# Adding x on GpSimd image by image, three images later, with each image stored alone

## What is computed

```python
g  = (x - mean) / sqrt(var + 1e-5)         # per image and channel (group norm with 32 groups of 1 channel)
xd = concat(g[..., 0::2, 0::2], g[..., 0::2, 1::2], g[..., 1::2, 0::2], g[..., 1::2, 1::2])  # 128 x 32 x 32
feats = concat(dwconv1x1(xd), dwconv3x3(xd), dwconv5x5(xd))   # depthwise, 3 x 128 channels
y   = einsum('bchw,oc->bohw', feats, w_proj)                  # 384 -> 128 channels
out = x + interleave(y)                                        # the inverse of the step to xd
```

## Time and profile before

| | us |
|---|---|
| median of 3 runs (lowest to highest) | 147.44 (147.08 to 148.12) |
| the profiled execution | 148.02 |
| its span, first to last instruction | 146.2 |
| busy: PE / DVE / POOL / ACT | 129.3 / 125.1 / 111.5 / 109.1 |
| granted TensorE clock, mean of the span | 0.955 of full |

### The profile page before, as it was taken

The page is one execution under the profiler, slowest core; times in us unless marked ns, Lnnn a source line. Parts: engine busy times, 40 slices in busy tenths (PEclk is TensorE's granted clock), DMA queues, the critical chain, the costliest instruction groups (busy, mean ns, idle before and its releaser), DMA issues.

```text
span 146.2 us, 1541 instructions
## 1 busy us (share of the span) xinstructions
PE 129.3 (88%) x507; PEld 97.5 (67%) x507; DVE 125.1 (86%) x153; ACT 109.1 (75%) x113; POOL 111.5 (76%) x81
## 2 busy tenths in 40 slices
PE   5963999999999999999999999999999996996500
PEld 5941878887877677767776777677766773783200
DVE  7467838989999999999999999999999999997700
ACT  1377973999999999999999999899989970500000
POOL 6110686979999999997989998999999999992000
PEclk9998579999999999999999999999999999999965
DMA  3999999707034034025019995700399920094997
GB/s 72 255 241 197 198 206 209 118 15 141 2 76 78 0 74 83 0 57 95 0 31 184 205 194 116 152 0 0 72 215 173 209 57 0 4 215 97 200 192 157
DMA packets 35799, 16.78 MB, mean 115 GB/s; under 512 B 34000, under 2 KB 34128, under 8 KB 35408
## 3 DMA queue, kind: packets, MB, share of 16 engines
q1 hardware_dynamic: 30928, 8.67, 31.0%
q0 software_dynamic: 1440, 7.04, 24.8%
q10 hardware_dynamic: 3424, 0.98, 3.3%
HBM read 5.46 MB, written 4.19 MB: 66 GB/s over the span
## 4 chain that ended last, share of the span: by engine, by line
PE 55%; DVE 17%; POOL 8%; DMA 7%; ACT 3%; issue 3%; ACTq 1%; DVEq 0%; POOLq 0%
PE YP L665 49%; DVE ACC L592 11%; POOL RING_SUM L316 7%; DMA X<-in_x_dram 7%; PE YP L716 6%; DVE F L602 3%; DVE ACC L584 2%; DVE ACC L596 2%; ACT HI L382 2%; ACT Y L413 1%; ACT PROD L430 1%; POOL LO L303 1%; DVEq L95 0%; DVE X L626 0%; ACTq L217 0%
## 5 line engine op out<-in xcount | busy, mean ns | idle before, releaser
L316 POOL TENSOR_TENSOR RING_SUM<-RING_SUM,PROD 128x900 f32<-128x900 f32 (+1 forms) x44 | 89.1, 2037 | 5.1 <-ACT PROD L430 0.8
L592 DVE SCALAR_TENSOR_TENSOR ACC<-G,coef,ACC 128x930 f32<-128x930 f32 (+1 forms) x60 | 71.6, 1194 | 1.9
L430 ACT ACTIVATE PROD<-G,coef 128x900 f32<-128x900 f32 (+1 forms) x44 | 43.7, 1057 | 0.0
L665 PE MATMUL YP<-HI,whi 128*128 128x512 f32 (+1 forms) x144 | 38.8, 425 | 3.1 <-ACT HI L382 3.1
L665 PE MATMUL YP<-HI,wlo 128*128 128x512 f32 (+1 forms) x144 | 38.3, 419 | 0.0
L665 PE MATMUL YP<-LO,whi 128*128 128x512 f32 (+1 forms) x144 | 36.9, 407 | 0.0
L665 PEld LDWEIGHTS YP<-HI,whi 128*128 128x128 f32 x144 | 29.1, 204 | 11.5 <-ACT HI L382 3.0
L665 PEld LDWEIGHTS YP<-HI,wlo 128*128 128x128 f32 x144 | 27.3, 190 | 9.2 <-issue 2.9
L665 PEld LDWEIGHTS YP<-LO,whi 128*128 128x128 f32 x144 | 27.2, 190 | 7.7 <-issue 1.0
L392 ACT ACTIVATE G<-X,nbias,rstd 64x1024 f32<-64x1024 f32 x16 | 21.1, 1318 | 3.8 <-DVE nbias L503 3.2
L413 ACT ACTIVATE Y<-YP 64x1024 f32<-64x1024 f32 x14 | 15.3, 1091 | 7.0 <-PE YP L716 6.7
(11 more groups left out here) (61 smaller groups left out, 64.3 us busy)
## 6 DMA issues: line engine op xcount, KB each, us to landing
LO<-G POOLq DMA_DIRECT2D x7, 543.0 KB, 4.9
X<-in_x_dram SPq DMA_DIRECT2D x14, 256.0 KB, 5.4
X<-Y POOLq DMA_DIRECT2D x3, 1024.0 KB, 7.0
out_dram<-X SPq DMA_DIRECT2D x12, 256.0 KB, 4.7
out_dram<-X SPq DMA_DIRECT2D x6, 128.0 KB, 3.1
XS<-in_x_dram SPq DMA_DIRECT2D x2, 256.0 KB, 4.3
X<-in_x_dram ACTq DMA_DIRECT2D x2, 256.0 KB, 8.2
XS<-in_x_dram SPq DMA_DIRECT2D x1, 512.0 KB, 8.1
```

The lines of the kernel that those rows point to most:

```text
L316: pool.tensor_tensor(dst, dst, prod(b, k), ALU.add).then_inc(prod_added, 1)
L430: act.activation(prod(b, k), g_tap(b, POOL_OF[b][k + 1]), ACT.Copy, scale=of5(POOL_OF[b][k + 1])).then_inc(prod_ready, 1)
L592: dve.scalar_tensor_tensor(part(ACC, tap), g_tap(b, tap), of5(tap), part(ACC, tap), ALU.mult, ALU.add).then_inc(acc_step, 1)
L665: mm = nc.tensor.matmul(dst, w[:, n, :], src, start=start, stop=False, skip_group_check=True)
```

## The change

One accumulating DMA for each of the images 0 to 5 (64 partitions, 512 KB) takes the place of one for each of three pairs (128 partitions, 1024 KB). Image b is added behind the first ring addition of image b+3, for b = 0 to 4; image 5 behind ring addition 4 of image 7. SP waits for each image and stores it alone; the number and the size of its stores stay. ACT's wait ahead of `copy_y(b)` is for image b-4.

```diff
-ADD_X_AT = [(4, 2), (6, 2), (7, 6)]
+ADD_X_AT = {(b + AREAS, 0): b for b in range(B - AREAS)}
+ADD_X_AT[(7, 4)] = 5
...
-        row_added = [sem(f"row_added{t}") for t in range(PAIRS - 1)]
+        row_added = [sem(f"row_added{b}") for b in range(B - 2)]
...
-            for t in range(PAIRS - 1):
-                sp.wait_ge(row_added[t], 16)
-                store(2 * t, 0, PH)
-                store(2 * t + 1, 0, PH)
+            for b in range(B - 2):
+                sp.wait_ge(row_added[b], 16)
+                store(b, 0, PH)
...
                     if (b, k) in ADD_X_AT:
-                        add_x(ADD_X_AT.index((b, k)))
+                        add_x(ADD_X_AT[b, k])
...
-            def add_x(t):
-
-                pool.wait_ge(y_copied, 4 * (t + 1))
-                pool.dma_start(X[:, t, :, :].rearrange("p h w -> p (h w)"),
-                               Y[:, t % 2, :, :, :].rearrange("p h w j -> p (h w j)"),
-                               accum_op=ALU.add).then_inc(row_added[t], 16)
+            def add_x(b):
+
+                p0, t = HALF * (b % 2), b // 2
+                pool.wait_ge(y_copied, 2 * (b + 1))
+                pool.dma_start(X[p0:p0 + HALF, t, :, :].rearrange("p h w -> p (h w)"),
+                               Y[p0:p0 + HALF, t % 2, :, :, :].rearrange("p h w j -> p (h w j)"),
+                               accum_op=ALU.add).then_inc(row_added[b], 16)
...
                 if b >= 4:
-                    act.wait_ge(row_added[b // 2 - 2], 16)
+                    act.wait_ge(row_added[b - 4], 16)
```

## The result

The changed kernel took 142.5 us in the median of 4 runs (142.16 to 144.3), the kernel before 147.26 on the same occasion: ratio 0.967, 95% interval 0.959 to 0.976. The forecast was 143.4 and its range began at 142.5, so that the median is a hair outside (142.495). Timed twice more on other occasions, the changed kernel took 143.51 us against 147.6 (6 runs; ratio 0.972, 0.966 to 0.978) and 143.36 against 147.34 (6 runs; 0.976, 0.969 to 0.983). The ratios are taken over the runs within 1.5% of the fastest of their kernel, the medians over all runs, so that the two can differ by up to 1% where a kernel's runs spread wider than that. The direction and the cause were right.

A forecast was written before the change was run, and what follows sets the result against it. SP's backlog of ten stores, released late by the third accumulation, was taken to bound the kernel. Last issue 138.8 + landing 3.0 + closing 0.4 = 142.2 us against 146.2; median 147.44 - 4.0 = 143.4, range 142.5 to 144.9.

The forecast's parts named there:

- What bounds the kernel before: At the end, SP's ten stores, released by the third accumulation at 133.5 us; for 7.5 us only stores run.
- Image 4 leaves the end: Image 4's accumulation, issued at 114.0 us, lands 118 to 121, so its two stores go while SP is idle.
- Image 5: Its accumulation, issued behind image 7's fifth ring addition at 122.4 us plus POOL's delay, lands 4.8 later, at 127.9.
- the first rival: SP's backlog only shrinks: issues cost POOL 1.1 us, half the partitions take 7.0; gain 1.8, median 145.6; chance 0.07.
- The end: Last store issue at 138.8 us, landing 3.0, closing 0.4: span 142.2 against 146.2, 4.0 us less.
- What POOL pays: Six accumulation issues instead of three, 0.7 us each: delay 1.4 at POOL's last ring addition, under 6.7 of slack.
- Against the runs: For the whole kernel, the 4.0 us gain taken off the earlier median of 147.44 gives 143.4.
- The landing term: At the kernel's end, 256 KB stored by SP and ACT together: landing taken as 3.0 us, bounds 2.3 and 4.0.
- the third: Rival: software-issued DMAs hold POOL, whose halves of image 6 set the end; at 2.5 us each, median 151.0; chance 0.03.

The follow-up runs named there:

- the late POOL: Changed kernel with four more POOL additions into a scratch tile ahead of image 7's ring additions: median 150.4 us, ratio 1.020 (1.012 to 1.028).

## Why the prediction was right, and where it was wrong

*What bounds the kernel before*: right. SP's stores, released by the last accumulation, set the end. Moving that one DMA earlier gains, moving image 5, or image 4 with image 5 behind it, back loses, and shortening DVE gains nothing until the backlog is gone.

*Image 4 leaves the end*: right, with stores at 121.52, half a microsecond later than the latest named. Both parts carry: with image 5 late the end is 5.4 us behind DVE, with image 4 late 6.0 (image 5 lands 3.9 us later there too), with the pair in one DMA at image 5's place 4.9, with both placed by the change 3.2.

*Image 5*: the issue at 123.5 was right (122.4 plus POOL's delay and the later start). The landing was mis-sized. The row I took as nearest had the same bytes but other partitions; 4.8 us was taken, 7.7 measured for this one, above the upper bound of 7.0 too. It cost nothing, because SP still had 1.7 us of pause ahead of image 7. The whole pair's 7.0 of the earlier trace rows, which I had taken as the bound only and which the first rival used, was the nearer value: 7.1 to 7.9 was measured for an image issued alone. Ahead of the result no row showed a transfer of 64 partitions, so that both values were estimates, and the runs show these times, not what makes them.

*The end*: 3.0 us of landing were taken for the last issue; they were 2.5 and 2.8. With the closing instructions 3.2 us instead of 3.5 from DVE's end. This makes the gain 4.3 instead of 4.0.

*What POOL pays*: right, 0.7 for an issue and 1.3 in all, with 5.3 us of slack left.

*Against the runs*, and the range taken from it: this is the step that failed. The gain was taken off the median of three runs, and for the spread of the runs the lower end was moved by only 0.2 us, from 142.7 to 142.5, although the prediction names a spread of 1 us, as if the rest of the kernel stood still. The landing term, mis-sized by 0.3, isn't enough: 147.44 - 4.3 is 143.1. What the runs showed in its place is a start of the first `F` that moves by about 2 us in either kernel (42.0 to 44.4 in the three profiles of the changed kernel, 42.5 to 44.4 in the four of the kernel before and its variants). The spans of the changed kernel go from 140.2 to 142.5, and those of the kernel before, in 23 runs of the last occasion, from 143.3 to 147.2. The first four runs had three of the early kind (140.4 to 140.9), hence 142.5; with two and three of six the larger samples gave 143.5 and 143.4. These lie on the forecast partly by luck, since 147.6 and 147.34 less 4.3 are 143.3 and 143.0.

The change itself doesn't visibly make the early kind more frequent. Take as early a span that puts the first `F` before 43 us, which is under 145.5 us for the kernel before and under 141.2 for the changed one. On the last occasion these are 11 of 23 and 3 of 6 runs, on the one with the first repeat 4 of 11 and 2 of 6. All engines also have the same program up to image 3 in both kernels. So the three of four in the first sample look like the draw of a small sample, which these counts support and don't prove.

*The rivals*: none came true as a whole. Half of the first did, the landing of 7.0 or more, but not its price of 1.1 for an issue, so that SP was free in time. The weakness of the third shows in the late POOL: I had the end follow POOL's halves of image 6, and it followed image 5's accumulation.

## What to carry to other kernels

When the span goes on for several microseconds after the last computing, follow the store queue back to the DMA or addition that released it, and ask what could have been released earlier; moving one issue by two steps was worth 2.5 us of 147 here. Half the partitions took as long as all (7.2 us for 512 KB, 7.0 for 1024 KB), so splitting an accumulation by partitions paid here only where the pieces could go at different times; a piece of half the rows over all partitions landed in 4.6 us, but no kernel here was faster by it. Take the spread that a profile's early stretch allows into the range, even where the change doesn't touch it.

## What the runs showed of the hardware

- An SBUF accumulation of 512 KB landed in 7.2 us over 64 partitions and in 4.6 over 128; two of 64 partitions, issued 0.6 us apart, landed 5.1 us apart.
- The same accumulation landed later behind ring addition 4 of image 7 than behind addition 6: 7.6 to 7.9 us against 7.1 for 512 KB over 64 partitions, 8.4 against 6.9 for 1024 KB over 128.
- TensorE's granted clock in the stretch from 18 to 22 us was 0.62 in one execution and 1.00 in another of the same kernel, and DVE's first `F` and all behind it came 2.3 us later; whether by the clock alone isn't shown.
- A store of 128 KB beside one other landed in 2.5 to 2.8 us.
